# Three-layer decoder on one core: where the transposes of the middle layers and of the first norm's rows stand on TensorE

## What is computed

```
x = layernorm(x + linear_attention(x))        # decaying state, 128 wide
x = layernorm(x + cross_attention(x, ctx))    # 16 heads of 16, softmax
x = layernorm(x + self_attention(x) + moe(x)) # 16 heads of 16; 8 experts, the best 2 weighted
```

## Time and profile before

| | us |
|---|---|
| median of 3 runs (1268.46 to 1268.57) | 1268.56 |
| the profiled execution, whole | 1266.94 |
| its span, first to last instruction | 1265.0 |
| PE busy | 1220.8 |
| DVE busy | 902.8 |
| ACT busy | 771.1 |
| POOL busy | 366.0 |

### The profile page before, as it was taken

One profiled execution on the slowest core, in us unless ns is written; L12 is line 12 of the kernel. 1 busy time (PEld: TensorE's weight loads), 2 busy tenths in 40 slices (PEclk: granted clock), 3 DMA queues, 4 the chain that ended last, 5 costly groups with the idle time before them and its releaser, 6 DMA issues.

```text
span 1265.0 us, 19962 instructions
## 1 busy us (share of the span) xinstructions
PE 1220.8 (96%) x6936; PEld 601.8 (48%) x6936; DVE 902.8 (71%) x1836; ACT 771.1 (61%) x1072; POOL 366.0 (29%) x471
## 2 busy tenths in 40 slices
PE   8889999999999999999999999999999999999998
PEld 4433444544555445454554545454454534544443
DVE  2577886677777787777776777767877787667772
ACT  2255556666675765756657665666657576655664
POOL 6410103211621134320522206221153204430261
PEclk9899999999999999999999999999999999999999
DMA  7825034313233342233333143332223333303300
GB/s 254 135 43 94 18 52 68 51 29 76 50 69 52 51 85 42 51 45 70 68 67 61 20 74 68 68 52 45 51 42 51 52 52 52 68 2 52 52 19 18
DMA packets 50243, 74.92 MB, mean 59 GB/s; under 512 B 8536, under 2 KB 20320, under 8 KB 49888
## 3 DMA queue, kind: packets, MB, share of 16 engines
q1 hardware_dynamic: 48896, 72.72, 32.8%
q10 hardware_dynamic: 1248, 0.92, 0.4%
HBM read 18.04 MB, written 4.19 MB: 18 GB/s over the span
## 4 chain that ended last, share of the span: by engine, by line
PE 83%; DVE 7%; ACT 5%; issue 3%; DMA 1%; ACTq 0%; POOL 0%; SPq 0%; DVEq 0%
PE ms L451 38%; PE op L451 17%; PE sc L451 15%; PE mx L451 9%; DVE maxes L928 3%; ACT probs L759 2%; PE ms L557 2%; PE ms L502 1%; ACT moe L752 1%; PE ms L552 1%; DMA qs<-q_parts 1%; DMA w_ident<-in_ident 1%; DVE k_parts L838 0%; ACT x L777 0%; DVE heads L901 0%
## 5 line engine op out<-in xcount | busy, mean ns | idle before, releaser
L928 DVE TENSOR_REDUCE maxes<-mx 128x1 f32<-128x512 f32 x1024 | 657.4, 683 | 215.3 <-PE mx L451 213.4
L759 ACT ACTIVATE probs<-sc 128x1024 f32<-128x1024 f32 x512 | 524.3, 1024 | 373.8 <-PE sc L451 368.3
L1131 POOL TENSOR_TENSOR x<-x,moe 128x256 f32<-128x256 f32 x256 | 187.4, 732 | 687.0 <-ACT moe L752 666.5
L451 PE MATMUL op<-probs,v 128*32 128x512 f32 x2048 | 273.6, 606 | 2.9 <-ACT oT L697 2.5
L451 PE MATMUL sc<-qs,ks 50*128 50x512 f32 x1024 | 256.7, 497 | 11.9 <-ACT probs L759 10.3
L451 PEld LDWEIGHTS sc<-qs,ks 50*128 50x128 f32 x1024 | 95.4, 183 | 308.4 <-ACT probs L759 231.5
L451 PE MATMUL mx<-ks,qs 48*128 48x512 f32 x1024 | 209.0, 402 | 10.9 <-DVE maxes L928 8.9
L752 ACT ACTIVATE moe<-ms,comb 128x256 f32<-128x256 f32 x256 | 106.8, 472 | 22.1 <-PE ms L451 22.1
L451 PEld LDWEIGHTS mx<-ks,qs 48*128 48x128 f32 x1024 | 97.7, 187 | 20.8 <-DVE maxes L928 14.7
L451 PE MATMUL ms<-we_hi,x2T_hi 128*128 128x512 f32 x256 | 93.7, 447 | 2.5 <-DVE shift_r L892 1.3
L451 PEld LDWEIGHTS op<-probs,v 128*32 128x32 f32 x2048 | 40.5, 108 | 96.4 <-issue 95.0
(11 more groups left out here) (131 smaller groups left out, 1264.8 us busy)
## 6 DMA issues: line engine op xcount, KB each, us to landing
ks<-k_parts SPq DMA_DIRECT2D x192, 128.0 KB, 4.2
qs<-q_parts SPq DMA_DIRECT2D x189, 128.0 KB, 4.6
xT_s<-in_xT SPq DMA_DIRECT2D x8, 512.0 KB, 3.8
x_s<-in_x SPq DMA_DIRECT2D x8, 512.0 KB, 4.0
ctxT_s<-in_ctxT SPq DMA_DIRECT2D x8, 512.0 KB, 4.2
out<-x SPq DMA_DIRECT2D x7, 512.0 KB, 2.9
qs<-shift_r SPq DMA_DIRECT2D x128, 8.0 KB
probs<-in_we SPq DMA_DIRECT2D x1, 1024.0 KB, 7.1
```

What stands on the lines that cost most here:

```text
L451: return nc.tensor.matmul(dst, lhsT, rhs, start=first, stop=last, skip_group_check=True)
L759: nc.scalar.activation(probs[:, (2 * s + h) % 3, :, :], sc[:], ACT.Exp).then_inc(exp_out, 1)
L928: nc.vector.tensor_reduce(maxes[:, g % 2, at:at + 1], mx[:, i % 3, :], AX_X, ALU.max).then_inc(max_out, 1)
L1131: nc.gpsimd.tensor_tensor(x2[:, n % 2, t, :], x2[:, n % 2, t, :], moe[:, k % 2, j * D:j * D + D], ALU.add).then_inc(acc, 1)
```

## The change

Two edits. `hT1` of `MID_LONG` moves from the second half of slot 20 to the first. And `soon` becomes true for `hT0`, `hT1`, `x2T0`, `x2T1` of every batch and for `x0`, `x1` of batches 3 to 7; `first_out` is written out so that it stays as it was.

```
-MID_LONG = {"hT0": (20, 0), "hT1": (20, 1), "cy0": (21, 1), ...
+MID_LONG = {"hT0": (20, 0), "hT1": (20, 0), "cy0": (21, 1), ...
...
 def soon(task, n):
-    return task in ("hT0", "hT1", "x2T0", "x2T1") and n in (0, B - 1)
+    return task in ("hT0", "hT1", "x2T0", "x2T1") or task in ("x0", "x1") and n >= 3
...
 def first_out(task, n):
-    return soon(task, n) or task in ("k3c0", "q3c0") and n in (0, B - 1)
+    return task in ("hT0", "hT1", "x2T0", "x2T1", "k3c0", "q3c0") and n in (0, B - 1)
```

More of the change, by code:

```diff
@@ L65 @@
        "x_bias": (-27, 0), "x1_bias": (7, 0), "load_xT": (-31, 0), "load_x": (-17, 1), "load_ctx": (-1, 0)}
-MID_LONG = {"hT0": (20, 0), "hT1": (20, 1), "cy0": (21, 1), "cy1": (22, 1), "x2T0": (27, 0), "x2T1": (28, 0),
+MID_LONG = {"hT0": (20, 0), "hT1": (20, 0), "cy0": (21, 1), "cy1": (22, 1), "x2T0": (27, 0), "x2T1": (28, 0),
             "gate": (29, 0), "gateT": (31, 0), "combT": (33, 1), "be0": (36, 0), "be1": (37, 0), "k3c0": (34, 0), "q3c0": (35, 1),
```

## The result

The changed kernel takes 1291.24 us (median of 4 runs, 1287.89 to 1293.26) against 1268.57 before: 22.7 us more, a ratio of 1.0179 with a 95% interval of 1.0158 to 1.0201. The forecast was 1283.3 with a range of 1274 to 1289. The direction and the place are right, the size is a third too small, and the median lies above the range.

What follows compares the result with a forecast made beforehand. PE's own list was taken to bound the kernel, so reordering only adds or removes short waits. Terms of 13.0 (hT), 1.2 (x) and 0.5 (x2T) gave 14.7 us over 1268.56, so 1283.3 us, range 1274 to 1289.

Steps and rivals of the forecast that it cites:

- part 1: hT0 and hT1, batches 1 to 6: hT1 waits for qc0, moe11 for hT0's copy; 2.17 us a batch, 13.0 in all.
- the split of 1.43 and 0.74: At hT: 1.43 us new wait for hT0's copy; 0.74 for scores and maxima leaving a wait's shadow, and the product's neighbour.
- Part 2: x0 and x1, ten units: no wait changes hands, the dearer switch to scores costs 0.12 us each, 1.2 us in all.
- four transposes followed by scores take 0.53 us: Price on PE from the start of four transposes to the start of the scores, used for the moved units: 0.53 us.
- The cover of `op`'s copy: At x0 and x1: ACT's copy of `op` still ends before `values` wants it, with 0.38 us left.
- Part 3: x2T0 and x2T1, twelve units: qc1 and q1 start as before, no cost; only batch 6 loses 0.5 us, once.
- The covers of part 3: Slack at x2T0 and x2T1 before qc1 and q1 would be delayed: 0.21 us at x2T0, 0.12 to 0.38 across x and x2T.
- the sum of 22.5 us: Alternative total if each transpose cost about 275 ns, four 1.10 us: 22.5 us in place of 14.7, 1291 us.
- The sum: Whole kernel: 13.0 + 1.2 + 0.5 = 14.7 us slower, 1283.3 us.
- the granted clock: Rival, chance 0.01: in the slot where PE stands still twice, the clock falls to 1.2 GHz; up to 24 us, near 1307.
- Half as slow: Rival, chance 0.08: hT1 waits for qc0 but moe11's wait for the copy is hidden; 6.1 us, 1274.7 us.
- Slower still: Rival, chance 0.07: late ACT uses up covers at the 22 x and x2T units, some 0.25 each; 5.5 us, 1288.8 us.

## Why the prediction was right or wrong

**What bounds the kernel, and part 1: right.** PE's list is the bound and hT is the place. The low part of qc0 did not move, hT1 waited for it ahead of the scores, and the product then waited for the copy. Forecast 2.17 us a batch, measured 2.24; the split of 1.43 and 0.74 was measured as 1.44 (by taking the copy's wait away) and 0.80. Of the 0.07 missing 0.05 are the price of four transposes followed by scores, 0.58 here (392.75 to 393.33) for 0.53, see below. Nothing gave it back later, as said.

**Part 2: right in kind, too small.** 0.19 us a unit in place of 0.12, 1.9 us in place of 1.2. The step that failed is the price "four transposes followed by scores take 0.53 us": it was read where a product stood ahead. Behind `values`, which is where all ten go, it is 0.59. The cover of `op`'s copy held.

**Part 3: right.** Eleven units at nothing, 0.58 us at the twelfth, for 0.5.

**The rule weighed.** Four transposes did not cost 1.10 us, the estimate by the 275 ns of the page "TensorE: Matmul & The Clock Gate" of the Trainium skill (Part 4: PE-mode transpose), but 0.59. The covers of part 3 held, and that the sum of 22.5 us came near the result is luck. It was not even that estimate's own sum: at 0.57 more for each the ten x0 and x1 would have added 5.7 us, which it leaves out.

**The sum: the step that failed is what it left out.** By its own steps it gives 14.7 us, and the order alone cost 15.9. The rest of the 22.7 is the granted clock, and that stood among the rivals with a chance of 0.01. Two things were wrong there. The evidence against it was a stretch of the kernel before with eight transposes and 0.6 us of standstill in 63, which says nothing on a slot with two standstills; and the question to ask was whether any place in the kernel before stands still for as long as slot 20 would. There is one, slot 29 with 1.66 us. In the profiled execution it kept its clock, so that this trace alone would not have warned; of the 12 later profiles with the same standstill 8 had the clock low behind it. Where the longest runs of the kernel before lose their clock (0.985 in 8 of 67) no trace shows. It is more than slot 29 has lost in any trace: 0.985 over 1275 us is, by working back, some 38 us at the lower level, against 10.2. The price was off too: I took the whole slot at the lower level, 4 us a batch, near 1307. Measured, a fall costs 1.3 to 1.5 us as a rule and once 4.2, and comes in three or four of six batches: 4 to 9 us in each of three profiled runs.

That the clock and not a dependency is the rest is shown from two sides. With the waits in place but PE kept busy, either standstill filled, every batch costs 2.21 to 2.25 us. And at an equal granted clock the kernel with the first standstill filled is 15 to 16 us above the kernel before, as the order alone gives: at 0.995, on the same chip, 1284.5 us against 1268.7 to 1269.0, and at 0.999 1279.8 and 1279.9 against 1264.1 to 1264.9 on the two other chips.

The page "TensorE: Matmul & The Clock Gate" of the Trainium skill says in Part 4: PE-mode transpose that a transpose does not count as busy for the clock in the same way. Slot 20 has eight of them between and beside its standstills, so that the trace does not speak against it, but no run here replaced them by other matmuls. It stays open how much they took part. They are not needed for a fall: in slot 29 the last ones stand over 10 us ahead of it (187.07 and 199.07 us in the kernel with the copy moved first), and the clock fell there too. Nor are two standstills of this length always enough: between 1125 and 1161 us every trace has one of 0.53 to 0.55 and one of 1.3 us with 2.1 us of work between them, and none of the 14 shows a fall there.

**The rivals.** "Half as slow" is in effect the kernel with the copy moved first; it did not happen by itself. "Slower still" named a cause that did not occur. The median of 1291.24 is 2.2 us above the range, which ended at a rival whose price was given without the clock.

## What to carry to other kernels

On an engine that is the bound, work moved ahead of a stage that feeds the others carries its waits with it: ask first what its buffer waits for, and then whether what comes after waits for an engine that has just been held up. Then add up how long TensorE stands still there in all, and set it against places of the kernel that stand still as long, in more than one run: standstills like the two of slot 20 can cost the clock as well. Where such a wait can't be removed, a matmul that nobody needs, of less than the wait's length and into a free bank, kept the clock up here at no cost.

## What the runs showed of the hardware

- The granted clock can fall to 1.2 GHz in the middle of a run that is 96% busy on PE, after standstills of 0.66 and 1.37 us with four transposes, scores and maxima between them (11 of 18 batches in three traces), and at another place after a single one of 1.66 (8 of 13 traces). With one of the two filled it held in all six batches of both traces. At a third place it fell in 2 of 14 traces behind 0.29 us alone.
- The same program has a different mean granted clock in different runs, and its time goes with it at some 0.94 us for each 0.001. A fall behind slot 20 lasted 3.4 us in ten cases and 10.2 us in one.
- Four fp32 transposes of 128x128 take 0.41 us up to a product, 0.53 up to scores if they stand behind a product, 0.59 if they stand behind `values`. A matmul of 128 rows by 384 fp32 columns takes 0.64 us, in two instructions of 0.32 each, not the 0.33 that I had expected.
